# A four-layer transformer stack on eight cores: integer casts moved to the middle stage, feed-forward weights loaded in pieces, and mixes of neighbouring tokens issued at other points

## The reference

```
L0 attn: Q,K,V = X@Wq+bq, X@Wk+bk, X@Wv+bv; S = tril(Q K^T)/32; A = softmax(S)
         out[q,:] = (sum_k A[q,k]) * V[q,:]
L0 ffn:  xr = mu_r*x + (1-mu_r)*x_prev ; xk = mu_k*x + (1-mu_k)*x_prev   (x_prev: token before)
         out = sigmoid(xr @ W_r^T) * (relu(xk @ W_k^T)^2 @ W_v^T)
L1 attn: 16 heads of 64, full softmax attention, gelu, @ Wpost, + X
L1 ffn:  integer weights (int32, -127..127): h = silu(x@wg^T) * (x@wu^T);  out = h @ wd^T
```

## Time and profile before

| | us |
|---|---|
| runs shown | 3481.66, 3648.88, 3765.32 (median 3648.88) |
| the profiled execution | 3484.66 |
| its span (slowest core, core 0) | 3483.5 |
| spans of the eight cores | 3457.6 to 3483.5 |
| PE busy | 3162.8 (91%) |
| ACT busy | 1854.3 (53%) |
| DVE busy | 1514.3 (43%) |
| POOL busy | 648.2 (19%) |

### The profile page before, as it was taken

The page is one execution under the profiler, slowest core; times in us unless marked ns, Lnnn a source line. Parts: engine busy times, 40 slices in busy tenths (PEclk is TensorE's granted clock), DMA queues, the critical chain, the costliest instruction groups (busy, mean ns, idle before and its releaser), DMA issues.

```text
span 3483.5 us, 50592 instructions; the slowest of 8 cores (3457.6 to 3483.5 us)
## 1 busy us (share of the span) xinstructions
PE 3162.8 (91%) x17670; PEld 1287.4 (37%) x17670; DVE 1514.3 (43%) x2452; ACT 1854.3 (53%) x1948; POOL 648.2 (19%) x1115
## 2 busy tenths in 40 slices
PE   5998886999999997779999999999999999999798
PEld 2444332443444432223333333333333333333333
DVE  2555565655665432243343343343344344344332
ACT  1443323333333327876676776676676676676421
POOL 1444433321223220010030030020020120120211
PEclk9999897999999999989999999999999999999999
DMA  7588747223332223623333343244243244243232
GB/s 163 128 186 165 188 110 166 95 86 91 103 106 82 82 100 97 154 91 125 114 128 116 108 138 119 95 138 128 92 137 127 88 138 132 87 139 113 74 116 94
DMA packets 192424, 412.79 MB, mean 118 GB/s; under 512 B 49584, under 2 KB 74160, under 8 KB 191024
## 3 DMA queue, kind: packets, MB, share of 16 engines
q1 hardware_dynamic: 180144, 369.70, 32.8%
q0 software_dynamic: 12032, 39.85, 8.0%
HBM read 357.06 MB, written 104.86 MB: 133 GB/s over the span
## 4 chain that ended last, share of the span: by engine, by line
PE 75%; DMA 7%; DVE 6%; ACT 6%; issue 4%; POOL 2%; DVEq 0%; SPq 0%; ACTq 0%; POOLq 0%
PE ps L1268 10%; PE ps L1316 10%; PE ps L1280 10%; PE ps L713 9%; PE ps L706 7%; PE p_t L1100 6%; PE ps L1081 6%; PE p_n L1103 5%; ACT c_pt L95 4%; PE ps L473 3%; PE ps L517 2%; PE p_n L417 2%; DMA a_wkT<-l_wkT 1%; DMA s_x<-r_xt 1%; DMA r_xa<-x 1%
## 5 line engine op out<-in xcount | busy, mean ns | idle before, releaser
L95 ACT ACTIVATE c_pt<-ps,negm 128x1024 bf16<-128x1024 f32 x1024 | 1075.7, 1111 | 230.1 <-PE ps L1083 229.1
L1100 PE MATMUL p_t<-c_pt,c_v 128*64 128x512 bf16 x2048 | 410.0, 397 | 5.1 <-DVE c_pvs L1114 4.6
L1081 PE MATMUL ps<-c_q,c_k 64*128 64x512 bf16 x1024 | 332.4, 386 | 83.8 <-ACT c_pt L95 72.7
L1103 PE MATMUL p_n<-c_pt,ones 128*64 128x512 bf16 x2048 | 398.4, 385 | 0.0
L1316 PE MATMUL ps<-c_wd,c_hh 128*128 128x512 bf16 x1536 | 351.4, 382 | 23.1 <-DVE c_o L1206 21.0
L1268 PE MATMUL ps<-c_h,c_wg 128*128 128x512 bf16 x1536 | 366.2, 381 | 1.2 <-DVE c_h L213 0.9
L1280 PE MATMUL ps<-c_h,c_wu 128*128 128x512 bf16 x1536 | 364.7, 380 | 0.0
L1083 PE MATMUL ps<-c_q,c_k 64*128 64x512 bf16 x1024 | 334.6, 389 | 0.0
L1274 DVE SCALAR_TENSOR_TENSOR c_th<-c_th,ps 128x512 f32<-128x512 f32 x192 | 132.1, 688 | 457.7 <-ACT c_th L95 457.7
L151 POOL TENSOR_SCALAR c_pof<-c_pof 128x1 f32<-128x1 f32 x32 | 6.6, 207 | 1440.0 <-DVE c_pof L144 1440.0
L95 ACT ACTIVATE c_th<-ps 128x512 f32<-128x512 f32 x192 | 114.6, 597 | 279.8 <-PE ps L1268 277.1
(11 more groups left out here) (191 smaller groups left out, 4353.8 us busy)
## 6 DMA issues: line engine op xcount, KB each, us to landing
c_wg<-s_wg SPq DMA_DIRECT2D x192, 256.0 KB, 2.8
c_wu<-s_wu SPq DMA_DIRECT2D x192, 256.0 KB, 3.2
s_x<-r_xt SPq DMA_DIRECT2D x64, 512.0 KB, 3.7
c_k<-s_k SPq DMA_DIRECT2D x64, 512.0 KB, 4.6
c_v<-s_v SPq DMA_DIRECT2D x64, 512.0 KB, 5.5
r_xa<-x SPq DMA_DIRECT2D x32, 512.0 KB, 8.7
r_xt<-x SPq DMA_DIRECT2D x32, 512.0 KB, 5.3
r_xa<-s_x SPq DMA_DIRECT2D x32, 512.0 KB, 5.4
```

The source lines that it names most:

```text
L95: return self.ACT.inc(self.nc.scalar.activation(*a, **k))
L1081: nc.tensor.matmul(bank[:, 0:512], k_[0:64, tc * 128:(tc + 1) * 128], q_[0:64, :], start=True, stop=True, tile_position=(0, 0))
L1100: nc.tensor.matmul(p_o[hd * 64:(hd + 1) * 64, :], v_[:, tc * 128 + hd * 64: tc * 128 + (hd + 1) * 64], p[:, hd * 512:(hd + 1) * 512], tile ...
L1103: ins = nc.tensor.matmul(p_l[hd * 64:(hd + 1) * 64, :], B.ones[:, 0:64], p[:, hd * 512:(hd + 1) * 512], tile_position=(0, hd * 64), **fl)
```

## The change

1. `weight_casts` is no longer called after tiles 2 to 25 of A1. It is called after each `f_tile` of groups 0 to 5 of A2.
2. `f0_wkT` and `f0_wvT` were each loaded by one DMA of 4 MB (f32) after tile 15. They are loaded in 8 pieces of 512 KB each, two after each of the tiles 16 to 19 (`f0_wkT`) and 20 to 23 (`f0_wvT`). `f0_wrT`, one DMA after tile 27 before, comes in 8 pieces, two after each of the tiles 28 to 31.
3. `prep1` of group 0 was called once in each of the tiles 24 to 27; it is called twice in each of 24 and 25.
4. The first `mix` "k" was emitted in a row after tile 27; it is spread at 1.7 from 9 us after tile 25. The first `mix` "r", in a row after tile 28, is spread at 2.4 from there.
5. In A2, `mix(G + 1, "r")` has a gap of 2.3 instead of 1.7, and `mix(G + 2, "k")` is called after `qk(G, True, 3)` instead of after `qk(G, True, 1)`.

```diff
@@ tile_step
-        elif 24 <= T < 28:
-            A2.prep1(0, T - 24)
+        elif T < 26:
+            A2.prep1(0, 2 * (T - 24))
+            B.after(5.0, lambda: A2.prep1(0, 2 * (T - 24) + 1))
@@ phase_a1, the loop over tiles
-        if T == 15:
-            A2.load("f0_wkT", [t_sc[15]])
-            A2.load("f0_wvT", [t_sc[15]])
-        if 2 <= T < 2 + HC:
-            B.weight_casts(T - 2)
-        if T == 27:
-            A2.load("f0_wrT", [B.g_done])
-            A2.mix(0, "k", 0.0)
+        if 16 <= T < 24:
+            for c in range(2):
+                A2.load("f0_wkT" if T < 20 else "f0_wvT", [t_sc[15]], 2 * (T % 4) + c)
+        if T >= 28:
+            for c in range(2):
+                A2.load("f0_wrT", [B.g_done], 2 * (T % 4) + c)
+        if T == 25:
+            B.after(9.0, lambda: A2.mix(0, "k", 1.7))
         if T == 28:
             A2.xr_free = t_sc[27]
-            A2.mix(0, "r", 0.0)
+            A2.mix(0, "r", 2.4)
@@ PhaseA2.load
-        self.w_tok[nm] = B.slot("d" + nm).dma(B.nc.gpsimd.dma_start(
-            out=self.dst[nm][:].rearrange("p (c d) -> p c d", d=D),
-            in_=self.W[nm].rearrange("(c p) d -> p c d", p=128)))
+        out = self.dst[nm][:].rearrange("p (c d) -> p c d", d=D)
+        src = self.W[nm].rearrange("(c p) d -> p c d", p=128)
+        if c is not None:
+            out, src = out[:, c:c + 1, :], src[:, c:c + 1, :]
+        self.w_tok[nm] = B.slot("d" + nm).dma(B.nc.gpsimd.dma_start(out=out, in_=src))
@@ PhaseA2.run
                 if G == 0:
                     self.prep1(1, ti)
+                if G < 6:
+                    B.weight_casts(4 * G + ti)
...
-                self.mix(G + 1, "r", 1.7)
+                self.mix(G + 1, "r", 2.3)
...
-                if p == 1 and G < 6:
+                if p == 3 and G < 6:
                     B.until(self.tr1, 4 * G + 11)
                     self.mix(G + 2, "k", 2.2)
```

More of the change, by code:

```diff
@@ L634, in __init__, with load @@
         self.t_mu = B.slot("dMu").dma(B.nc.sync.dma_start(out=self.mu[:], in_=W["f0_mu"]))
-    def load(self, nm, need):
+    def load(self, nm, need, c=None):
         B = self.B
         B.POOL.wait(*need)
-        self.w_tok[nm] = B.slot("d" + nm).dma(B.nc.gpsimd.dma_start(
-            out=self.dst[nm][:].rearrange("p (c d) -> p c d", d=D),
-            in_=self.W[nm].rearrange("(c p) d -> p c d", p=128)))
+        out = self.dst[nm][:].rearrange("p (c d) -> p c d", d=D)
[3 more added lines that the diff above has]
+        self.w_tok[nm] = B.slot("d" + nm).dma(B.nc.gpsimd.dma_start(out=out, in_=src))
     def t2_take(self):
```

## The result

| | before | after |
|---|---|---|
| median of the runs side by side, us | 3486.23 | 3460.22 |
| ratio, with its 95% interval | | 0.9931 [0.9909, 0.9953] |
| the profiled execution, us | 3484.66 | 3460.22 |
| mean span of its eight cores | 3472.0 | 3453.2 |

The changed kernel is faster by 0.7%. The forecast was 3446, or -39 us; the two profiled executions differ by 24 us, and their cores by 19 in the mean. The median of 3648.88 ahead of the prediction came from disturbed executions; all ratios here leave such out.

A forecast was written before the change was run, and what follows sets the result against it. PE's waits in the 1325 us ahead of stage B were taken as the bound. Terms -25 - 13 + 12 + 3 - 16 + 0 = -39 against 3484.66 gave 3446 us, own range 3425 to 3466, wider range 3415 to 3490.

The forecast's parts named there:

- Term 4: Start of A2: old waits of 12.6 and 10.7 us stay, four new casts lengthen the DMA traffic; +3 us (0 to +12).
- Term 1: A1 around 365 us: weight pieces and moved casts remove the 25.2 us wait for a late input tile; -25 us.
- Term 2: First mixes, end of A1: spreading them removes PE waits of 7.0 and 3.5 us and the low clock; -13 us.
- Term 3: End of A1: PE waits 9.5 us for the last pieces of f0_wrT, then 2.5 us of low clock; +12 us.
- Term 5: Groups 1 to 6 of A2: waits of 3.9 us fall to 2.3 to 2.6, clock partly kept; -16 us.
- the halves: Value products, groups 1 to 6: the clock stays up or not, taken half and half, 2.5 x 6 / 2 = 7.5 us.
- Rival (a): All six later groups: low clock goes with the waits, shorter DVE queue helps ACT too; -68 us, 3417; chance 0.15.
- The casts beside A2: Groups of A2: each moved cast costs POOL about 0.6 us, covered by waiting for DVE's statistics; 0 on the path.
- Rival (c): Groups of A2: casts clog SP, slow stores delay loads, 14 us in each of six groups; 3530 us; chance 0.10.
- The rule weighed in the prediction: Casts beside a busy DVE in A2: exclusive shared port slows their issue, up to 6 x 1 us where it counts.
- (b): A1 input tiles: pieces do not cure the late tile, waits of 3 to 4 us leave 15 us; 3461; chance 0.15.
- (d): End of A1: f0_wrT pieces queue and land at 535, +26 instead of +12, casts cost 12; 3469 us; chance 0.10.

## Why the prediction was right, and where it was not

The direction was right and the time was even in the narrower range of 3425 to 3466, near its upper end: 39 us were forecast, 24 came on the slowest cores and 19 in the mean of the traced ones. That it held is in part luck. Term 4 came out at +17, beyond its own bound of +12, term 1 had the wrong cause, and the other errors were small. By the steps of the prediction:

**Term 1 (-25).** The size was right: the wait at 365 us and its low clock are gone, and no load of an input tile between 288 and 370 us takes over 6.1 us. The cause was not. The prediction put the late tile down to "two whole weights and a cast per tile" and gave the cure to both edits. The trace of before has the last packet of the weights at 329.1 us; for the last 30 of its 36.9 us POOL's queue had only casts, in packets of 4.7 us (79.1% of 16 x 22 us, over 59). What the weights did was to pile up six casts behind them. The casts alone moved take 28.7 us off A1, and with them gone the pieces take off nothing (471.4 us whole, 472.4 in pieces). With the casts in place the pieces take off 9.9. So the step that failed was to count the weights and the casts alike, by their megabytes. In the engines' time they are near each other (an estimate from the packets: 1 MB of a weight's f32 is 256 packets of 0.23 us, 3.7 us of all 16 engines; 1 MB of a cast's int32 is 16 packets of 4.4 us, one on each), but beside the long packets SP's queue moved a sixth.

**Term 2 (-13).** The size was right beside the moved casts. From the kernel with the casts alone moved to the one with whole loads A1's end goes from 483.7 to 471.4 us, -12.3. (They differ in A1 by the first mixes and by `f0_wrT` in pieces; the waits of 7.0 and 3.5 us stand in the one and not in the other.) It is not a term of its own, though: with the casts in A1 it is -4.7, since the doubled `prep1`, costed at DVE's 2.2 us each, asks for its tiles sooner than SP delivers them. The prediction followed that step to DVE and not to the DMA behind it.

**Term 3 (+12).** Right: a wait of 9.5 us was forecast, 9.9 measured (9.3 to 11.0 over the cores), released by the DMA of `b_fr`. The two pieces took 6.95 us from the issue of the second, between the 5.0 and the 10.0 of the rows it was taken from, and the first product after it took 5.84 us instead of 3.62, so 12 in all. It was also avoidable: one tile earlier there is no wait.

**Term 4 (+3).** This is the failed one: +16 in the wait (12.2 to 28.3 in the mean) and +17 in all, 14 of the 20 us by which the mean gain fell short of the sum. The prediction said that the casts lengthen the traffic "from about 573 us", where the loads have slack. They lengthened it where the load of the residual tile lay. "Both hang on the first `f_tile`, which moves as a whole" was wrong too: `f_tile` moved 10 us against the weights, which POOL issues without waiting for PE. So term 3 and the casts together caused term 4, and the terms were costed as if apart. Behind that stands one more false step: the queue's own order was looked at, not the engines below it. The Trainium skill ("DMA: Bandwidth & Descriptors", SWDGE vs HWDGE vs iDMA) says that the two kinds of queue feed different queues inside each DMA engine, which takes turns between them. The trace agrees as far as SP's queue goes on beside POOL's, and shows how unequal the shares are: 39.4% of the engines' time and 129 GB/s beside the weights, 5.9% and 21 GB/s beside the casts, whose packets take 4.4 us where a weight's take 0.23. Casts that stood behind the weights reached the engines at 528.8 us, and the load that was then on its way lasted until they were done. Why one packet of a cast takes 4.4 us is shown by no run.

**Term 5 (-16).** The mechanism was right, the size was -12. ACT is last, as forecast, and the wait fell from 3.85 to 3.05 us, not to 2.3 to 2.6: 4.8 us in all instead of 8.4. The clock was kept in 7 of 48 cases instead of 1, which is 0.6 us a group in the value products, 3.6 in all, not the 7.5 of the halves. The remaining 4 us of the 12 are not located. Rival (a), the clock that stays up, did not come at waits of 3.05 us; at the gap of 3.4, with waits of 1.9 us, it came in 46 of 48.

**The casts beside A2 (0).** Right in groups 1 to 5. Whether casts run in groups 0 to 5, in 1 to 6 or not at all beside A2, group 0 to group 7 takes the same (650.2, 650.1 and 650.8 us). With the old gap it is 664.8 with the casts there and 662.4 without; the kernel with the first mixes alone, which touches none of these groups, lies as far off (660.1). Rival (c) set its price from a store of over 8 us. Between 600 and 1200 us the stores of the changed kernel landed in 7.4 us at most (4.5 in the median, against 2.7 before), and the casts themselves in 8.1 at most. From the trace of the changed kernel, L1441 between 600 and 1250 us:

```profile
L1441 POOL DMA_DIRECT2D s_wu<-f_wu x10: 605/609/613, 649.3 to 1050.7; - x10
...
DMA to landing us min/median/max: 5.0/6.2/8.1
```

In the whole kernel before they took 0.605 us to issue at the median, so they are issued no slower beside the mixes. The rule weighed in the prediction cost nothing here. It was read too widely: the Trainium skill ("SBUF — State Buffer", Who interferes with whom) reports that a `tensor_copy` on DVE was seen to stall DMAs and a `tensor_tensor` not, and the trace agrees for the `tensor_tensor` and `scalar_tensor_tensor` instructions of the mixes.

**Rivals (b) and (d).** Neither came. (b) asked whether pieces cure the tile: alone they leave 21.8 us of waits, but with the casts gone it did not matter. (d) asked for late pieces of `f0_wrT`, and they came on time; the large loss was one step further on.

**What stays open.** From group 7 to the end the changed kernel takes 5 us more in the mean (2220.4 against 2215.3), though no edit touches stage B. It is not chance alone: the ten kernels with the larger gap have 2217.8 to 2221.5 there, the kernel before and the three others without it 2214.7 to 2216.7. About 1 us of it lies in the value products of group 7 (28.1 against 27.2); the cause of the rest is not shown.

## What to carry to other kernels

Before a wait is costed, ask what does not wait with it: here POOL went on issuing 12 MB of weights while PE stood for 10 us, and the next load met that traffic 12 us later in its course, for 16 us more. When bulk traffic is moved, look for the small load on the path that it will lie across, and move either one: the last pieces one tile earlier were worth 22 us. Weigh bulk traffic by the time of one of its packets, not by its megabytes alone. And take apart edits that are argued from one wait: with the casts moved, the pieces did nothing, and the spread mixes were worth 12 us with the casts out of A1 and 5 with them in it.

## What the chip showed that I had not expected

- DMA engines that were busier moved less: 96% busy at 173 GB/s with the casts (DRAM to DRAM, int32 to bf16) in the mix, 81 and 84% busy at 210 and 206 GB/s without.
- The packets of a cast were of 32 KB and took 4.4 us (4.7 in A1 of before); those of an f32-to-bf16 weight load were of 2 KB and took 0.23 us. Beside casts another queue moved 21 GB/s, beside weights 129.
- A load of 512 KB took about 13 us when it was issued 34 to 36 us behind three 4 MB weights, 11.1 at 48.5 us without casts, and 29.1 at 46.6 us with casts queued behind the weights; in the later groups the median is 3.7 us.
- What a wait cost in TensorE's clock turned on a microsecond. Over the fourteen traces, in groups 1 to 6 of all cores, the 64 value products stayed under 14.1 us, near their time at the full 2.4 GHz, in 7 of 192 cases behind waits of about 3.9 us, in 76 of 384 behind 3.0 us and in 86 of 96 behind 1.9 us. In the mean they took 15.6, 15.0 and 14.1 us.
